# Output network of a graph and LSTM kernel: the next tile's turn, the gate and one hinge change their places

## The reference, cut to what matters

```
t         = max over d of (x[d] + Wt[f, d]) + bt[f]
cvx       = max over 8 pieces of (t * sl_cvx[f, p] + of_cvx[f, p])
ccv       = min over 8 pieces of (t * sl_ccv[f, p] + of_ccv[f, p])
trop      = s[f] * cvx + (1 - s[f]) * ccv,          s = sigmoid(alpha)
classical = gelu(x @ Wc + bc)
g         = sigmoid(x @ Wg + bg)
out       = (g * trop + (1 - g) * classical) @ Wd + bd
```

## Time and profile before

| | us |
|---|---|
| median of 3 runs | 6146.52 |
| lowest and highest run | 6146.45 to 6148.37 |
| profiled execution | 6148.58 |
| its span, first to last instruction | 6146.8 |
| TensorE busy (matmul) | 5497.9 (89%) |
| VectorE busy | 4964.1 (81%) |
| ScalarE busy | 3352.9 (55%) |
| mean granted TensorE clock | 0.958 |

### The profile page before, as it was taken

The page is one execution under the profiler, slowest core; times in us unless marked ns, Lnnn a source line. Parts: engine busy times, 40 slices in busy tenths (PEclk is TensorE's granted clock), DMA queues, the critical chain, the costliest instruction groups (busy, mean ns, idle before and its releaser), DMA issues. The chain is left out here.

```text
span 6146.8 us, 107920 instructions
## 1 busy us (share of the span) xinstructions
PE 5497.9 (89%) x31674; PEld 3582.1 (58%) x31674; DVE 4964.1 (81%) x9353; ACT 3352.9 (55%) x6537; POOL 1704.9 (28%) x3544
## 2 busy tenths in 40 slices
PE   9998999999899917999999994876758999999999
PEld 6666777777788815666666663543434444444444
DVE  8995444444699978999999996986858999999998
ACT  6664444444455505666666662221217878788787
POOL 3331000000254414566656662267350000000000
PEclk9999999999999969999999996997979999999999
DMA  4441000000355521222222221256352222221221
GB/s 137 136 136 54 0 0 0 0 0 0 110 177 176 174 91 62 74 72 72 73 76 72 72 72 35 86 183 234 117 190 88 68 84 82 69 84 66 88 84 48
DMA packets 359539, 528.54 MB, mean 86 GB/s; under 512 B 28000, under 2 KB 298080, under 8 KB 359424
## 3 DMA queue, kind: packets, MB, share of 16 engines
q1 hardware_dynamic: 323120, 401.16, 20.1%
q0 software_dynamic: 36304, 126.13, 6.0%
HBM read 298.06 MB, written 229.13 MB: 86 GB/s over the span
## 5 line engine op out<-in xcount | busy, mean ns | idle before, releaser
L1766 PE MATMUL t_fetched<-t_wpart,t_onehot 128*128 128x512 f32 x4096 | 1221.8, 420 | 35.9 <-DVE t_tout L1871 16.0
L1871 DVE SCALAR_TENSOR_TENSOR t_tout<-t_fetched,t_top,t_tout 128x1024 f32<-128x1024 f32 x896 | 1149.0, 1282 | 36.3 <-PE t_fetched L1766 5.1
L1766 PEld LDWEIGHTS t_fetched<-t_wpart,t_onehot 128*128 128x128 f32 x4096 | 691.7, 188 | 269.2 <-DVE t_tout L1871 131.2
L2704 DVE SCALAR_TENSOR_TENSOR f_line<-f_hinge,f_vec,f_line 128x1024 f32<-128x1024 f32 x512 | 655.0, 1279 | 79.4 <-ACT f_hinge L2582 48.0
L2194 PE MATMUL ts_fetched<-t_wpart,ts_onehot 128*128 128x512 f32 x1608 | 506.6, 449 | 166.0 <-ACT ts_onehot L2169 60.8
L604 PE MATMUL l_ps<-l_wih,l_x 128*64 128x128 f32 (+1 forms) x6144 | 544.6, 312 | 1.0 <-DVE l_ps L530 1.0
L572 ACT ACTIVATE l_act<-l_ps 128x128 f32<-128x128 f32 x1024 | 253.6, 276 | 526.0 <-PE l_ps L604 526.0
L2194 PEld LDWEIGHTS ts_fetched<-t_wpart,ts_onehot 128*128 128x128 f32 x1608 | 304.0, 207 | 317.3 <-DVE ts_tout L2262 187.4
L604 PE MATMUL l_ps<-l_whh,l_ht 128*64 128x128 f32 (+1 forms) x6144 | 488.2, 308 | 0.0
L2621 PE MATMUL f_psc<-f_x,f_wc 128*128 128x512 f32 x1024 | 483.1, 594 | 0.0
L2634 PE MATMUL f_pso<-f_fused,f_wd 128*128 128x512 f32 x1024 | 461.9, 594 | 23.1 <-DVE f_ox L2700 23.1
(11 more groups left out here) (388 smaller groups left out, 10761.9 us busy)
## 6 DMA issues: line engine op xcount, KB each, us to landing
t<-t_tout SPq DMA_DIRECT2D x128, 512.0 KB, 2.6
f_t<-t SPq DMA_DIRECT2D x64, 1024.0 KB, 5.3
g_adj<-in_adj SPq DMA_DIRECT2D x128, 256.0 KB, 3.2
g_adjt<-in_adjt SPq DMA_DIRECT2D x128, 256.0 KB, 2.8
t_x<-x_normalised SPq DMA_DIRECT2D x130, 128.0 KB, 2.4
g_x<-in_x SPq DMA_DIRECT2D x64, 256.0 KB, 2.8
x_kept<-g_x SPq DMA_DIRECT2D x64, 256.0 KB, 2.2
g_x<-x_kept SPq DMA_DIRECT2D x64, 256.0 KB, 2.8
```

Source lines behind the costliest of these rows:

```text
L1766: mm = pe.matmul(fetched[c % RING][:, h * CH:(h + 1) * CH], one_hot[g][:, c % GRP * P:(c % GRP + 1) * P], w_part[part][:, k, h * CH:(h + 1 ...
L1871: dve.scalar_tensor_tensor(t_out[j][:, :], column[:, :], value, t_out[j][:, :], ALU.add, ALU.max)\
L2704: dve.scalar_tensor_tensor(acc[:, :], source, column(u, "bend", k), acc[:, :], ALU.mult, ALU.add)\
```

## The change

`SURE` goes from 4 to 3, so one hinge of each tile is now among the spare ones. The semaphore `rest_ready` (the fourth sure hinge is written) becomes `spare_ready`, which every spare hinge raises; VectorE waits for it ahead of each spare bend, and TensorE waits for the last spare hinge ahead of a turn. TensorE reads the counts `before` for this from memory. TensorE's turn moves behind the products of the second half. ScalarE's gelu and tanh of the first half move ahead of the spare hinges.

```diff
-SURE = 4
+SURE = 3
...
                     wait_past(act, chained, q - 1)
                     begun = not (isinstance(q, int) and q == 0)
-                    for k in range(SURE - 1):
+                    for k in range(SURE):
                         act.activation(hinge[v][:, k, :], ps_t[:, :], ACT.Relu, bias=column(u, "knot", k))\
                            .then_inc(sure_ready, 1)
...
+                    wait_past(act, fused_ready, q - 1)
+                    gate(u, q, 0)
+
                     wait_past(act, chained, q)
                     with act.Fori(0, more[u]) as k:
                         act.activation(spare[:, ds(k, 1), :].rearrange("p o t -> p (o t)"), ps_t[:, :], ACT.Relu,
-                                       bias=column(u, "knot", k + SURE))
-                    act.activation(hinge[v][:, SURE - 1, :], ps_t[:, :], ACT.Relu, bias=column(u, "knot", SURE - 1))\
-                       .then_inc(rest_ready, 1)
-
-                    wait_past(act, fused_ready, q - 1)
-                    gate(u, q, 0)
+                                       bias=column(u, "knot", k + SURE)).then_inc(spare_ready, 1)
...
-            def turn(w, u, q, i_pairs):
+            def turn(w, u, i_pairs, spares):
...
-                wait_past(pe, rest_ready, q)
+                if spares is not None:
+                    pe.wait_ge(spare_ready, spares)
...
                     products(j, u, q, 0)
+                    products(j, u, q, 1)
+                    spares = before[FT] * m + before[u + 1]
                     if u < FT - 1:
                         w = (u + 1) // 2
-                        turn(w, u + 1, q + 1, 2 * m + w // 2 + 1)
+                        turn(w, u + 1, 2 * m + w // 2 + 1, spares)
                     elif not is_last(m):
-                        turn(0, 0, q + 1, 2 * m + 3)
-                    products(j, u, q, 1)
+                        turn(0, 0, 2 * m + 3, spares)
...
+            _, before = counts(pe)
             pe.wait_ge(w_ready, 8)
-            turn(0, 0, 0, 1)
+            turn(0, 0, 1, None)
...
-                    for k in range(SURE - 1):
-                        dve.wait_ge(sure_ready, (SURE - 1) * q + k + 1)
+                    for k in range(SURE):
+                        dve.wait_ge(sure_ready, SURE * q + k + 1)
...
-                    dve.wait_ge(rest_ready, q + 1)
-                    dve.wait_ge(chain, done + SURE - 1)
-                    bend(u, acc, hinge[v][:, SURE - 1, :], SURE - 1)
                     with dve.Fori(0, more[u]) as k:
+                        dve.wait_ge(spare_ready, before[FT] * m + before[u] + k + 1)
                         dve.wait_ge(chain, done + k + SURE)
                         bend(u, acc, spare[:, ds(k, 1), :].rearrange("p o t -> p (o t)"), k + SURE)
```

More of the change, by code:

```diff
@@ L2440, in stage_ffn @@
         t_turned, c_done, g_done, cls_ready, th_ready = sems("t_turned", "c_done", "g_done", "cls_ready", "th_ready")
-        sure_ready, rest_ready, chain, chained = sems("sure_ready", "rest_ready", "chain", "chained")
+        sure_ready, spare_ready, chain, chained = sems("sure_ready", "spare_ready", "chain", "chained")
         diff_ready, gated_ready, fused_ready = sems("diff_ready", "gated_ready", "fused_ready")
```

## The result

| | before | after |
|---|---|---|
| median, us (6 runs each) | 6146.49 | 6171.47 |
| lowest to highest | 6145.89 to 6148.37 | 6169.73 to 6175.91 |
| profiled execution, its span | 6148.58, 6146.8 | 6175.91, 6174.0 |
| mean granted clock | 0.958 | 0.952 |

The ratio of the times is 1.0041, with a 95% interval of [1.0028, 1.0053]: 25.0 us slower, beyond the 0.2% that can be told from no change. The forecast was 6167.5, 21 us slower.

A forecast was written before the change was run, and what follows sets the result against it. Two engines, TensorE and VectorE, were taken as close to the limit in the output network. 15 x 1.35 + 0 + 0.8 = 21 us on 6148.58 gave 6169.6, median 6167.5; range 6150 to 6185.

The forecast's parts named there:

- The counts and VectorE's relief: Output network: two bends a block go, in tiles 6 and 7 where VectorE already waits for TensorE; they bring nothing.
- Rival 4: Naive reading: two bends fewer save 2.9 us of VectorE a block, 44 us faster, 6103; chance 0.05.
- T0: Moment at which the turn of tile 0 of a block is through; T1, T2, T3 likewise for later tiles.
- T0 to T3: Time for three tiles of a block: 38.73 us before; forecast 39.72 at a full clock, 40.08 with its fall.
- The cycle of a tile: Per tile: spares begin at 7.66; six spares give a 3.5 us gap, three a short stall; plain tiles stay 11.18.
- VectorE and f_ox: Tile 1's output part waits 1.25 us for VectorE's f_ox at a full clock; 0.99 us more a block.
- Rival 3: Not slower: chained bends at 1.17 us instead of 1.47, f_ox released at T1 + 11.2; 6142; chance 0.14.
- The clock: Granted clock falls behind the new 3.5 us gap, losing 1.7 us of work; 1.35 us more a block.
- Rival 1: The clock holds behind the gap: 0.99 us a block, 15.7 us slower in all, 6162; chance 0.20.
- Rival 2: Clock falls longer, 2.4 us lost: 6178; with plain tiles held 0.3 us by the previous gelu, 6191; chance 0.14.
- The ends: Stage's start, with TensorE's 17 register loads: 0, between -2 and +1.5 us; stage's end: +0.8 us.

The follow-up runs named there:

- gap filled: Changed kernel plus four zero-weight products between tile 0's second half and turn 1 in every block but the first: 6171.71 us, ratio 1.0038.
- loads late: Changed kernel with TensorE's 17 count loads moved from ahead of the first turn to behind tile 0's first-half products: 6167.54 us, ratio 1.0034.
- after again: Changed kernel as it is, run once more on another chip: 6176.49 us, ratio 1.0044.

## Why the prediction was right

**The counts and VectorE's relief.** Two bends a block went, and in tiles 6 and 7 they brought nothing here. Rival 4 (6103) read the busy time alone. The old order shows that three sure hinges have a worth, only not through those two bends: VectorE's first bend in tile 0 stands at T0 + 2.44 and turn 1 at T0 + 11.66 with and without them, but the wait for the fourth hinge goes, f_ox comes 2.3 us earlier, turn 2 no longer stalls, and T0 to T3 falls by 2.2 (38.54 to 36.31, both written out).

**The cycle of a tile.** All steps came as worked out: spares at T0 + 7.65 (7.66), turn 1 at T0 + 13.84 (13.88) with a gap of 3.38 (3.5), turns 2 and 3 with 0.36 us idle in front and 0.6 to 0.7 more in the tile's length (T2 to T3 11.85; 11.78 forecast), plain tiles 11.18. The cause of turn 1's place is the one named: the tanh that waits for its product stands ahead of all spares, and the second half's products are used up before the turn. The kernel with the hinge in that wait is the test of it: one hinge moved into the wait, and turn 1 comes 0.96 us earlier. TensorE's register arithmetic for the new wait cost nothing that shows, as taken; its bound counted seven loop rounds, the code has six.

**VectorE and f_ox.** With a full clock the wait is 1.17 to 1.34 in 11 blocks for 1.25 (gap filled); with the fall it is gone in 14 of 15 blocks. Rival 3 wanted the chained bends at 1.17 us; they stand at 1.47, so its point, f_ox ahead of a full-clock output part, was never reached.

What the prediction's sum holds without saying so: at a full clock T0 to T3 is the release of the first output part by f_ox and what stands behind it, and not the gap at turn 1. Before, the release comes at T0 + 30.12 and T3 8.61 later; with the gap filled the release comes at T0 + 27.87, 2.25 earlier, but the second half of tile 2 now stands ahead of turn 3 as well, and T3 is 11.86 later: 1.0 us more. With the fourth hinge in the wait, turn 1 is 0.96 earlier and the release is at T0 + 27.87 all the same. In the old order with three sure hinges, written out, the release is at T0 + 27.66 and T3 8.6 later. The gap itself costs only the clock.

**The clock.** The gap of 3.38 us brought the fall in 14 of 15 blocks, 1.7 us of work lost each in 12 of them (3.4 in two), as read off two gaps in other stages. T0 to T3 was 40.05 on average for 40.08. That it is so close is in part luck: the 12 blocks with a fall of 1.7 have a mean of 39.92, since the fall in some of them began in the gap, where it costs nothing (0.3 of the 1.7 us in the block shown), and the two longer falls (40.99 and 41.28) make up for that and for the block without one (39.50). Other executions of this order gave 39.83 (loads late, and loop written out) and 40.00 (after again). Rival 1 (the clock holds) is out for the whole, though it held in some blocks of some executions; its number, 39.72, is what the filled gap gave. Rival 2's longer fall was seen in two blocks, and its hold of the plain tiles not at all in this kernel, but in the next: the one with four sure hinges pays just that, 0.45 a tile. Its condition was closer than I took it.

**The ends.** The end was +0.84 for +0.8. The start was the term mis-sized: 5.8 us for 0, outside its own range of -2 to +1.5. I allowed for TensorE's loads to push ScalarE's first line by 0 to 3 us, and the sum took 2.0; they pushed it by 3.4. Turn 1 came 12.88 behind the line (12.7 forecast). From turn 1 to turn 2 the forecast had 10.8 us (4635.6 to 4646.4), and it took 15.1 (4637.10 to 4652.23): tile 1's first product waited 2.88 us for the gelu of tile 0's second half, which the sum did not have, and ran at the 1.2 GHz level. With the loads late that wait is there too, at 2.88, and the distance is 13.25; so 1.9 of the 4.3 us are the clock and 2.4 the wait and the slow work that stay. Moved behind the first products, the loads give 5.4 us back, and the start is then 0.3 longer than before.

**The sum.** 15 x 1.35 + 0.8 = 21 was forecast; 15 x 1.365 + 0.8 + 5.8 = 27.1 are in the profile, whose spans differ by 27.2, and 25.0 in the medians. The forecast was near because the part that repeats was right and the part that was missed is small beside the range. What stays open: why the fall's place inside the block drifts from block to block, why it came twice as long in two of them, and why it did not come at all behind the same gap in others.

## What to carry to other kernels

When an instruction that waits moves ahead of others on its engine, price it by what those others feed: here one tanh held six hinges, a turn and the clock. Then look for the wait that ends last: here it was VectorE's f_ox, and moving a turn behind more products put more work behind that wait. A change of three parts may hide a good one; the third part alone, in the old order, was 0.4 to 0.6% faster, while all three together lost 0.4%. And a wait that swallows a delay elsewhere (the f_ox wait and the clock's fall) makes the cure of either worth little until both are cured.

## What the runs showed of the hardware that was not expected

- The length of one gap did not decide whether the granted clock fell. Behind the gap of 3.37 or 3.38 us at turn 1 it fell in 14, 9, 12 and 15 of 15 blocks in four executions (after, loads late, loop written out, after again). Behind 2.4 us there (fourth hinge in the wait) it fell in 12 of 15, behind 1.9 (four sure hinges) in 3 of 15. Behind waits for f_ox of 2.1 to 3.6 us it fell in ten blocks with four sure hinges and held in two (2.10 and 2.17); behind 2.6 to 2.9 with the fourth hinge in the wait it fell in six and held in two (2.68 and 2.72). It fell once behind 1.48 (gap filled, the block of 41.72). It held behind most gaps of 2.79 with the gate alone moved, and behind all of up to 1.58 in before's blocks 1 to 15. In two of after's blocks, and in eight with the turn alone moved, 3.4 us of work was lost instead of 1.7.
- 17 register loads by TensorE took 7.76 us in front of its first turn, as ScalarE's did (8.51); put behind queued products they left the stage's start 0.3 us longer.
- A jump of a loop left ScalarE idle for 2.06 to 2.35 us (0.27 in the other blocks) in the old order with three sure hinges, and not in before; there it is VectorE's first bend that comes 1.6 to 1.9 us later, and its wait for the fourth hinge hides that. One of the two queues that load instructions moved 102 packets there and in after, 78 in before; the other 38 and 37 (page, part 3: packets, MB, share; after and before):

```profile
q14 instruction: 102, 0.84, 0.0%
```

```profile
q14 instruction: 78, 0.64, 0.0%
```

The Trainium skill, page "Runtime: NRT & Kernel Launch", section "Instruction fetch mechanics", says that a taken branch to a page that is not held forces a fetch before the engine goes on. The rows agree in that the delay follows the jump and is gone with the loop written out; that it is the fetch was not measured by itself.
